# One subtraction of the input split moved from VectorE to GpSimd in a convolution-attention kernel

## What is computed

```python
q = einsum('oc,bcn->bon', Wq, xf) + bq          # 32 channels
k = einsum('oc,bcn->bon', Wk, xf) + bk          # 32 channels
v = einsum('oc,bcn->bon', Wv, xf) + bv          # 256 channels
att = softmax(einsum('bdi,bdj->bij', q, k) / sqrt(32), axis=-1)   # 4096 x 4096
out = gamma * einsum('bcj,bij->bci', v, att)
fused = einsum('oc,bcn->bon', Wf, concatenate([out, x], axis=1)) + bf
```

## Time and profile before

| quantity | us |
|---|---|
| median of three executions | 1976.95 |
| the profiled execution, its own time | 1977.79 |
| its span in the trace | 1976.0 |
| PE busy | 1958.5 |
| DVE busy | 1677.9 |
| ACT busy | 1731.2 |
| POOL busy | 1288.6 |

### The profile page before, as it was taken

One profiled execution on the slowest core, in us unless ns is written; L12 is line 12 of the kernel. 1 busy time (PEld: TensorE's weight loads), 2 busy tenths in 40 slices (PEclk: granted clock), 3 DMA queues, 4 the chain that ended last, 5 costly groups with the idle time before them and its releaser, 6 DMA issues.

```text
span 1976.0 us, 46307 instructions
## 1 busy us (share of the span) xinstructions
PE 1958.5 (99%) x15720; PEld 1925.2 (97%) x15720; DVE 1677.9 (85%) x2676; ACT 1731.2 (88%) x2313; POOL 1288.6 (65%) x577
## 2 busy tenths in 40 slices
PE   9999999999999999999999999999999999999999
PEld 8899999999889999999988999999998999999998
DVE  6888988887788889988678888889867888888896
ACT  7899999997888999999788999999978899999996
POOL 0477777778047777777705777777760677777775
PEclk9999999999999999999999999999999999999999
DMA  4311111110321111111032111111104111111111
GB/s 138 89 20 18 18 21 21 21 18 16 117 79 23 18 18 18 21 21 22 12 124 72 23 22 17 17 19 21 22 12 134 39 23 22 21 16 17 20 22 17
DMA packets 297815, 69.69 MB, mean 35 GB/s; under 512 B 280528, under 2 KB 281296, under 8 KB 297680
## 3 DMA queue, kind: packets, MB, share of 16 engines
q1 hardware_dynamic: 296864, 67.90, 15.9%
q10 hardware_dynamic: 816, 0.13, 0.0%
HBM read 34.41 MB, written 33.55 MB: 34 GB/s over the span
## 4 chain that ended last, share of the span: by engine, by line
PE 93%; DVE 3%; ACT 2%; issue 2%; DMA 0%; POOL 0%; SPq 0%; ACTq 0%; DVEq 0%; POOLq 0%
PE ps_o L404 73%; PE ps_s L396 11%; PE ps_p L281 5%; PE ps_o L281 3%; PE ps_s L298 1%; DVE top L636 1%; ACT queries L496 1%; ACT hi L475 0%; DMA raw<-wf1T 0%; ACT raw L481 0%; ACT hi L559 0%; DVE val_lo L740 0%; DVE lo L682 0%; ACT ps_p L566 0%; ACT val_hi L508 0%
## 5 line engine op out<-in xcount | busy, mean ns | idle before, releaser
L824 POOL TENSOR_TENSOR raw<-raw,top_m 128x1024 f32<-128x1024 f32 x508 | 1209.1, 2415 | 498.3 <-DVE raw L677 258.3
L682 DVE TENSOR_TENSOR lo<-ps_p,hi 128x1024 fp32r<-128x1024 f32 x512 | 622.5, 1216 | 159.8 <-ACT ps_p L566 153.1
L636 DVE TENSOR_TENSOR top<-ps_s,top 128x512 f32<-128x512 f32 x960 | 658.4, 686 | 58.4 <-ACT raw L481 10.1
L559 ACT ACTIVATE hi<-raw 128x1024 fp32r<-128x1024 f32 x508 | 539.6, 1062 | 146.5 <-PE ps_o L404 137.3
L404 PE MATMUL ps_o<-val_hi,hi 128*128 128x258 f32 x4096 | 660.8, 283 | 5.8 <-DVE val_lo L740 5.6
L404 PE MATMUL ps_o<-val_lo,hi 128*128 128x256 f32 x4096 | 653.3, 281 | 0.0
L404 PE MATMUL ps_o<-val_hi,lo 128*128 128x258 f32 x4096 | 599.3, 284 | 0.2
L481 ACT ACTIVATE raw<-ps_s 128x512 f32<-128x512 f32 x1024 | 553.6, 594 | 28.6 <-PE ps_s L396 1.9
L404 PEld LDWEIGHTS ps_o<-val_hi,hi 128*128 128x128 f32 x4096 | 563.0, 189 | 7.8 <-DVE val_lo L740 5.4
L404 PEld LDWEIGHTS ps_o<-val_lo,hi 128*128 128x128 f32 x4096 | 560.5, 189 | 0.0
L404 PEld LDWEIGHTS ps_o<-val_hi,lo 128*128 128x128 f32 x4096 | 538.5, 190 | 1.3 <-DVE lo L682 0.6
(11 more groups left out here) (64 smaller groups left out, 1020.6 us busy)
## 6 DMA issues: line engine op xcount, KB each, us to landing
xf<-x SPq DMA_DIRECT2D x32, 512.0 KB, 3.8
conv_d<-conv_st SPq DMA_DIRECT2D x64, 256.0 KB, 2.1
result<-conv_d SPq DMA_DIRECT2D x512, 32.0 KB, 1.9
out<-result SPq DMA_DIRECT2D x510, 32.0 KB, 1.6
raw<-wf2T SPq DMA_DIRECT2D x1, 256.0 KB, 5.3
raw<-wv SPq DMA_DIRECT2D x1, 256.0 KB, 4.0
raw<-wf1T SPq DMA_DIRECT2D x1, 256.0 KB, 5.6
raw<-wkqT ACTq DMA_DIRECT2D x1, 64.0 KB, 2.3
```

The lines of the kernel that those rows point to most:

```text
L559: nc.scalar.activation(hi[:, t % 2], raw[:, slot].rearrange("p j i -> p (j i)"), ACT.Exp, scale=SCALE).then_inc(hi_done, 1)
L636: nc.vector.tensor_tensor(top[:, new], scores, top[:, new if half else old], ALU.max).then_inc(max_done, 1)
L682: nc.vector.tensor_tensor(lo[:, t % 2], ps_p[:].rearrange("p h n -> p (h n)"), hi[:, t % 2].bitcast(F32), ALU.subtract).then_inc(lo_done, 1)
L824: nc.gpsimd.tensor_tensor(raw[:, slot], raw[:, slot], top_m[:, r].unsqueeze(1).broadcast_to((P, JQ, I)), ALU.subtract).then_inc(sub_done, 1)
```

## The change

The call of `split_x` in the body of every chunk is taken from DVE, and the same subtraction with the same operands is written into POOL's program, in the body of the same chunk. Chunk 0 of every image is still split by DVE.

```diff
@@ DVE, project @@
                 kq_lo(c, C)
                 if start:
                     setup_values()
-                split_x(C + 1, c + 1)
                 values_lo(0)
                 values_lo(1)
                 if c in BETWEEN:
@@ POOL, project @@
             def project(b, c, first):
                 if c == 0 and not first:
                     finish_image(b)
+                if c < CHUNKS - 1:
+
+                    pool.wait_ge(x_hi_done, b * CHUNKS + (c + 2))
+                    nc.gpsimd.tensor_tensor(lo[:, (c + 1) % 2], xf[:, (c + 1) % 2].rearrange("p k n -> p (k n)"),
+                                            hi[:, (c + 1) % 2].bitcast(F32), ALU.subtract).then_inc(x_split, 1)
                 if c == CHUNKS - 1:
                     pool.wait_ge(sub0_done, b + 1)
```

## The result

The changed kernel takes 1981.53 us (median of 16 executions, 1980.64 to 1982.21), the kernel before 1976.91 us (16 executions, 1976.35 to 1977.32). The ratio is 1.0023, with a 95% interval of 1.0016 to 1.0030: slower by 4.6 us. The profiled execution of the change took 1981.72 us, with a span of 1979.9 us, against 1977.79 and 1976.0 before.

A forecast was written before the change was run, and what follows sets the result against it. PE was taken to bound the kernel; chunks 1 to 6 cost nothing, and chunk 7 costs 1.25 us in each of 4 images, 5.0 us on 1976.95, giving 1982.0 us, in a range of 1979.8 to 1984.0.

The forecast's parts named there:

- What bounds the kernel: PE, busy 1958.5 of 1976.0 us; only PE's work or the few places where PE waits can change the time.
- Removal worth at most 0.6 us: Taking 28 splits off DVE frees 34.3 us of busy time but brings the first fold at most 0.15 us forward per image.
- POOL's 2.41 us, from the subtraction of the maximum: Each moved split on POOL takes 2.41 us, read from POOL's 128x1024 subtraction with float32 output (L824).
- that rival: POOL's split is slower for its float32r output; at 3.2 us the total would be 1992 us; chance 4%.
- the estimate of 2.25 us: Duration of POOL's split taken as half the skill's 4497 ns for 2048 float32 elements; the measured row was preferred.
- Chunks 1 to 6 covered, until POOL needs about 2.9 us: PE's own work hides these six POOL splits with 0.5 to 0.6 us left, so they cost nothing.
- PE 1.38 us late at chunk 7: PE's keys and queries of chunk 7 have no slack and start 1.38 us later, waiting for POOL's low part.
- The fold 1.25 us late, 5.0 us in all: DVE's first fold of chunk 7 starts 1.25 us late, all reaching PE's attention start, in each of 4 images.
- my low end: Total cost of 4.2 us, with POOL's start at 0.02 and its split at 2.376 us; the fold 1.05 late.
- Covered after all, or released before the recorded end: Chunk 7's lateness is swallowed (1976.4 to 1977 us) or POOL releases 0.3 us early (1980.8 us); together 20%.
- POOL and DVE hold each other up: POOL's split waits for DVE instructions: 1984.8 us, up to 1989.6 if chunks 1 to 6 lose too; chance 5%.
- The signs: Expected profile: PE waits for POOL only before chunk 7, about 1.4 us; DVE 34 us less busy; split-to-attention 13.9 us.

The follow-up runs named there:

- the small dose: Chunk 7 on DVE, chunks 1 to 6 on POOL, each preceded by an extra 192-column POOL subtraction: 1977.18 us against 1977.04 for the kernel before.
- the large dose: Chunk 7 on DVE, chunks 1 to 6 on POOL, each preceded by an extra 512-column POOL subtraction: 1991.74 us against 1977.04 for the kernel before.

## Why the prediction was right

The forecast was 1982.0 us in a range of 1979.8 to 1984.0; 1981.53 was measured. Point by point:

- **What bounds the kernel.** Right. The new wait is the only one of PE's that grew by a microsecond or more in all, and it stands where the chain left PE.
- **Removal worth at most 0.6 us.** It fits: 0.4 us measured with the low part left out, within the noise, and 0.12 to 0.16 us an image in its trace, 0.6 in all.
- **POOL's 2.41 us, from the subtraction of the maximum.** Right: 2.402 median. The float32r output costs nothing extra, so that rival falls. So does the estimate of 2.25 us from the Trainium skill, "GPSIMD Engine Reference", section on performance versus the Vector engine, which was 0.15 too low.
- **Chunks 1 to 6 covered, until POOL needs about 2.9 us.** Right in kind: 24 splits on POOL, no change. The edge of 2.9 was a little too near: the small dose, some 2.96 us of work in all, was still covered with 0.2 us to spare, and the two doses together put it at 3.1 us.
- **PE 1.38 us late at chunk 7.** Mis-sized: 1.16 us. The term that was off is POOL's start and hand-over. I took 0.19 us for the start, from the one place where POOL had waited for DVE; the new instruction starts 0.08 us after ACT's high part (552.39 + 1.06 to 553.53). In the program, a semaphore increment of POOL stands between wait and instruction at the old place and not at the new one, which I had not counted; that this makes the difference is argued, not tried. From POOL's end to PE it was 0.04 to 0.05 us and not 0.12, and at chunk 7 the instruction took 2.38 and not 2.41: 0.11 + 0.08 + 0.03 are the 0.22 us.
- **The fold 1.25 us late, 5.0 us in all.** It is 1.07 late in image 1, and PE's attention 0.99 to 1.09: 4.2 us by the trace, 4.6 by the medians. By the trace my low end, 4.2, was nearly exact and the value I took was too high; by the medians both are 0.4 away. Part of the low end is luck: it took 0.02 for the start and 0.12 for the hand-over, measured are 0.08 and 0.05, and the two errors nearly cancel. The path through ACT's queries, DVE's low queries and the fold was as written down: DVE was not the late one any more (1.13 us idle before its low keys), and the fold followed DVE's low queries without a gap.
- **Covered after all, or released before the recorded end.** Fell. PE starts after the recorded end each time, so the recorded end is the real one here.
- **POOL and DVE hold each other up.** Not in this change: the folds (median 686 ns, 690 before) and the low values (678 to 693 ns, 678 to 692 before) kept their times, as the instructions with a PSUM input did before. The median of the low values went from 681 to 691 ns, but it is 691 too where POOL makes no low part at all (the run without that of chunk 7), so POOL isn't the reason. By the Trainium skill, "SBUF — State Buffer", section "Who interferes with whom", only a DVE instruction with two SBUF inputs or in a two-port mode contends with a GpSimd instruction that reads SBUF, and the one that comes second waits for the whole of the first. The runs with two such instructions at once agree in who is held up: DVE was first by 0.04 to 0.05 us and kept its 0.69 us, POOL's grew. They do not agree in how much: it grew by 0.5 us, where the full overlap is 0.65. No run here explains the 0.15 us between them.
- **The signs.** PE's waits came as listed, 4 times for POOL and only at chunk 7, but 1.0 us each and not 1.4. DVE's busy time fell by 31.7 us and not 34, for the reason given with the page. The way from the end of ACT's last split to PE's first attention matmul in image 1 is 13.63 us (553.45 to 567.08) and not 13.9. It grew by 1.02, just above the 1 us below which the prediction called itself wrong; in image 2 it grew by 0.99.

The busy times of the page would have misled in both directions: DVE was freed of 32 us and POOL, at 65%, seemed to have room; but its relief was worth 0.6 us at most, and POOL's longer instruction sat in front of PE, the engine that bounds the kernel.

## What to carry to other kernels

When work moves to a slower engine that is mostly idle, ask for each instance how long the consumer's own work covers the result, and not how full the engines are: here six of seven instances had 0.7 us of room and cost nothing, and the seventh had none and cost everything. The instance whose consumer had been brought forward is the one to look at first, and letting the consumer use the late operand last won back 3.8 of 4.6 us with the work still on the slow engine. A step named in the chain of waits isn't worth its duration: taking DVE's split out altogether gave 0.15 us of 1.2 an image, because the next engine, ACT, was just behind.

## What the runs showed of the hardware

- A subtraction of 128x1024 with two SBUF inputs takes 2.40 us on POOL with a float32r output, as with float32 (2.41), against 1.22 us on DVE; 192 columns take 0.60 and 512 take 1.29 us.
- A DVE instruction with two SBUF inputs that starts just ahead of such a POOL instruction lengthens it: 1.29 to 1.79 us for 512 columns, 2.40 to 2.91 for 1024, each beside 0.69 us of DVE. In the other order DVE was the one that grew, 0.425 to 1.05 us: in the earlier trace rows it starts at 90.82, and POOL's own timeline has two subtractions back to back from 86.79 to 91.59.
- A matmul that PE starts after waiting for POOL has 0.50 us in the trace instead of 0.40, and the next one starts 0.34 us behind it instead of 0.23 (the large dose).
- In the chain of waits of the changed kernel, POOL has 3% and "issue" 6% of the span. That isn't time lost to POOL. The chain follows POOL back from chunk to chunk through its idle time, as in this piece of image 1, where POOL's own timeline says that it waited 5.59 us for ACT:

```profile
547.94 5.56 issue
...
553.53 2.39 POOL lo L841
555.92 0.04 issue
555.96 1.68 PE ps_p L281 x6
```
